# Moving the K projections three slots ahead in a three-pass attention stage, and one norm step on GpSimd ahead of a row of scatters

## The reference, cut to what matters

```python
scores = einsum('bthd,bshd->bhts', q, k * scale) + mask     # 16 heads of 8, mask: -10000 above the diagonal
context = einsum('bhts,bshd->bthd', softmax(scores), v)
for _ in range(3 - 1):
    context = _self_attention(context, k, v, mask)
out = context.reshape(B, S, 128) @ out_w.T + out_b
```

```python
w, idx = top_k(xf @ Wg, 2); w = softmax(w)
xhat = (xf - mean) * rsqrt(var + 1e-6)
h = relu((xhat * gamma[e] + beta[e]) @ W1[e] + b1[e]);  out = h @ W2[e] + b2[e] + xf
y = sum over the two chosen experts of w * out
```

## Time and profile before

| | |
|---|---|
| median of 3 runs | 4461.56 us (4457.56 to 4463.29) |
| the profiled execution: its own time | 4461.56 us |
| its span, first to last instruction | 4459.8 us |
| busy in the span: PE, DVE, ACT, POOL | 77%, 63%, 47%, 26% |
| mean granted TensorE clock | 0.867 of full |

### The profile page before, as it was taken

The page is one execution under the profiler, slowest core; times in us unless marked ns, Lnnn a source line. Parts: engine busy times, 40 slices in busy tenths (PEclk is TensorE's granted clock), DMA queues, the critical chain, the costliest instruction groups (busy, mean ns, idle before and its releaser), DMA issues. The chain is left out here.

```text
span 4459.8 us, 86703 instructions
## 1 busy us (share of the span) xinstructions
PE 3442.5 (77%) x30682; PEld 2229.3 (50%) x30682; DVE 2809.0 (63%) x7618; ACT 2089.4 (47%) x4656; POOL 1178.7 (26%) x2276
## 2 busy tenths in 40 slices
PE   5886888887888658739998989677982478869882
PEld 2443454463555338724454545344541456659872
DVE  4884675264887575537676777476756458955453
ACT  2664665223444435425666666453650134335551
POOL 2322221011111234530101010133320431234555
PEclk9987999797998679968999999788995599979996
DMA  5323331033220322221202021223312140122332
GB/s 95 56 32 55 54 56 24 15 94 44 36 37 14 57 70 67 74 49 25 45 20 41 24 38 28 38 51 55 58 29 62 50 122 19 51 69 86 90 82 63
DMA packets 317480, 231.40 MB, mean 52 GB/s; under 512 B 45379, under 2 KB 300960, under 8 KB 317004
## 3 DMA queue, kind: packets, MB, share of 16 engines
q1 hardware_dynamic: 304124, 199.36, 22.6%
q0 software_dynamic: 12928, 26.50, 2.0%
HBM read 68.43 MB, written 55.53 MB: 28 GB/s over the span
## 5 line engine op out<-in xcount | busy, mean ns | idle before, releaser
L1351 ACT ACTIVATE PT<-ps 128x512 f32<-128x512 f32 (+1 forms) x1600 | 812.0, 560 | 478.8 <-PE ps L1411 221.7
L1301 DVE TENSOR_REDUCE M<-ps 128x2 f32<-128x512 f32 x1024 | 655.3, 684 | 253.0 <-PE ps L1285 223.8
L1264 PE MATMUL ps<-SKB 49*128 49x256 bf16 (+2 forms) x3584 | 425.0, 276 | 150.2 <-DMA SKB<-HH 59.1
L1298 DVE TENSOR_REDUCE M<-ps 128x3 f32<-128x384 f32 x768 | 390.6, 550 | 190.4 <-PE ps L1282 125.4
L1446 PE MATMUL ps<-PT,VA 128*9 128x256 f32 (+1 forms) x7168 | 449.5, 370 | 1.4 <-ACT PT L1351 1.0
L3716 ACT ACTIVATE SKB<-ps,SKB 128x128 f32<-128x128 f32 x1032 | 294.6, 371 | 281.6 <-PE ps L3636 198.3
L1391 PE MATMUL ps<-SKB 51*128 51x256 bf16 (+2 forms) x3584 | 364.4, 268 | 63.1 <-DMA SKB<-MT 41.5
L3778 DVE COPY SKB<-SKB 128x1028 f32 (+1 forms) x258 | 186.0, 721 | 288.6 <-PE ps L3645 165.6
L1264 PEld LDWEIGHTS ps<-SKB 48*128 48x128 bf16 (+1 forms) x3584 | 138.0, 95 | 449.3 <-issue 161.9
L3645 PE MATMUL ps<-SKB 128*128 128x128 f32 x2064 | 288.8, 285 | 32.8 <-ACT SKB L3716 25.7
L3636 PE MATMUL ps<-SKB 128*128 128x128 f32 x2064 | 289.9, 286 | 0.0
(11 more groups left out here) (487 smaller groups left out, 6725.4 us busy)
## 6 DMA issues: line engine op xcount, KB each, us to landing
SKB<-HH SPq DMA_DIRECT2D x1224, 64.0 KB
SKB<-HH SPq DMA_DIRECT2D x576, 32.0 KB
PT<-L_sorted_rows SPq DMA_DIRECT2D x258, 64.0 KB
L_sorted_results<-SKB SPq DMA_DIRECT2D x258, 64.0 KB
SKB<-in_L3f_w SPq DMA_DIRECT2D x32, 256.0 KB
L_sorted_rows<-TV SPq DMA_DIRECT2D x2, 4032.0 KB, 29.2
SKB<-scratch SPq DMA_DIRECT2D x2, 2048.0 KB, 11.0
SKB<-in_L1f_w SPq DMA_DIRECT2D x16, 256.0 KB
```

The source lines that it names most:

```text
L1264: k = e.matmul(self.mx_bank(m + i)[:, o:o + n], K.QS[self.set(c)][64 * i:64 * i + rows, s, 256 * bb + 128 * qt:256 * bb + 128 * qt + 128], ...
L1298: k = e.tensor_reduce(K.M3[n % 2][:, hh, 0:3], mx[:, 0:384].rearrange("p (a k) -> p a k", a=3), axis=AX.X, op=ALU.max)
L1301: k = e.tensor_reduce(K.M3[n % 2][:, hh, 0:2], mx.rearrange("p (a k) -> p a k", a=2), axis=AX.X, op=ALU.max)
L1351: e.activation(K.PT[:, x % 4, n * i:n * i + n], self.st_bank(x, i)[:, 0:n], ACT.Exp, bias=0.0, scale=self.scale).then_inc(*self.exp.inc())
```

## The change

In the attention stage with three passes the K projection goes from 15 to 18 slots ahead of the chunk's first unit, and the copies of K from 12 to 15 slots ahead. All that hangs on these two numbers moves along: the projection and its read, the four instructions of the split, the 12 copies. Q and V stay. No other stage takes these branches (the other self attentions have rope, a gate or a cross part). In the experts stage `pool_root(e, 2)` is emitted ahead of the 24 scatters of part 1 and no longer behind the first 8. In the experts of layer L3 `normed` is false, and nothing changes.

```diff
-        self.Q, self.KP, self.V = ... else (-29, -27, -19) if gate else (-25, -15, -19)
-        self.QSTK, self.KSTK = (-26, -17) if cross else (-20, -12) if reps > 1 else (-14, -20) if gate else (-20, -14)
+        self.Q, self.KP, self.V = ... else (-29, -27, -19) if gate else (-25, -18, -19)
+        self.QSTK, self.KSTK = (-26, -17) if cross else (-20, -15) if reps > 1 else (-14, -20) if gate else (-20, -14)
...
         for _ in self.steps["pool"]:
             pass
+        if D.normed:
+            D.pool_root(e, 2)
         for h in (1, 2):
             begin, n = D.begins[h - 1], D.parts[h].tiles * top
             for i in range(n):
-                if D.normed and h == 1 and i == 8:
-                    D.pool_root(e, 2)
                 e.wait_ge(*self.xc.at(begin + i * min(n, D.parts[h - 1].NB - 1) // n))
                 self.pool_scatter(e, h, i)
```

More of the change, by code:

```diff
@@ L953, in __init__ @@
         self.OUT, self.TURN = self.OOS + 1, 6 if cross or gate else 5
-        self.Q, self.KP, self.V = (-30, -20, -13) if cross else (-29, -20, -19) if rope else (-29, -27, -19) if gate else (-25, -15, -19)
-        self.QSTK, self.KSTK = (-26, -17) if cross else (-20, -12) if reps > 1 else (-14, -20) if gate else (-20, -14)
+        self.Q, self.KP, self.V = (-30, -20, -13) if cross else (-29, -20, -19) if rope else (-29, -27, -19) if gate else (-25, -18, -19)
+        self.QSTK, self.KSTK = (-26, -17) if cross else (-20, -15) if reps > 1 else (-14, -20) if gate else (-20, -14)
         self.stack_slots = 3 if reps > 1 else 6
```

## The result

The changed kernel takes 4503.88 us, the median of 4 runs (4503.51 to 4506.82), against 4460.50 (4457.56 to 4463.29) of the kernel before in the same comparison: +43.4 us, a ratio of 1.0101, interval 1.0086 to 1.0115. The prediction had the sign, and in the attention stage the mechanism, but half the size: 4483, range to 4499. The profiled execution took 4495.31 us; in code that the change doesn't touch it was already 9.3 us ahead of the execution of before when the experts' blocks began, so stages are compared from their own starts. By the two traces the attention stage is 36.6 us longer from slot 32 to its last slot, and the stretch from the first block of the experts to slot 32 is 7.7 us longer.

What follows compares the result with a forecast made beforehand. It took the slot-by-slot round through PE, DVE and ACT, plus single stalls, to set the attention stage's pace. 17.9 + 2.1 + 0.9 - 1.2 + 1.7 = +21.4 on 4461.6 gave 4483 us; range 4477 to 4491, with rivals 4471 to 4499.

Steps and rivals of the forecast that it cites:

- the odd chunks: Attention stage: K's projection, three slots ahead, waits for DVE where it waited for ACT; 0.3 us each, +0.9 us.
- the start: Start of the attention stage: copies of chunk 1's K follow the first 36 without a gap and land sooner; -1.2 us.
- the moved root: Experts stage: all 24 scatters follow the root back to back, so the last, which releases block 23, is late; +1.7 us.
- DVE's seed: Experts stage: the root on POOL waits for this seed until 1699.96, so moving it ahead gives no gain.
- the landing: Attention: context 7's copies land 18.5 us after Q's, holding PE at slot 120 and in two other groups; +17.9 us.
- the clock: Attention stage: two stalls a group lower the granted clock; 0.7 us for each group, +2.1 us.
- three groups, even chunks, with the clock: Attention stage: PE held until context 7 lands in three groups, 17.9 us, plus 2.1 us for the lower clock.
- The first stall: Attention, slot 112: the context's `hi` waits some 8 us for Q's copies; alone it makes PE some 3.5 us late.
- the upper bound of 1.41: Experts stage: scatter pitch in us if DVE's SBUF copies hold back GpSimd's descriptors; the root term would be +3.3 us.
- Rival C: Attention: Q's copies land before slot 112, so neither split waits and three stalls go; -12.4 us, 4449 us; chance 4%.

Runs made afterwards that it cites:

- 8.0 alone: Against the kernel before, K's projection and copies three slots ahead for chunks 3, 5 and 7 only: +8.0 us (ratio 1.0024).
- 9.6 and 14.2 alone: Against the kernel before, only the root moved ahead of all 24 scatters, run on two chips: +9.6 us (1.0027) and +14.2 us (1.0031).
- even chunks' kernel: Against the kernel before, K's projection and copies three slots ahead for chunks 2, 4 and 6 only: +27.7 us (ratio 1.0073).
- The run with Q ahead: Changed kernel's K move, root as before, Q of chunks 2, 4, 6 projected, split and copied 8 slots earlier: +27.0 us (1.0052) against the kernel before.

## Why the prediction was wrong

The steps on the mechanism held: the wait passed from K to the context, two slots earlier; the context landed behind 24 copies; PE was held at slots 120, 216 and 312; the odd chunks, the start and the moved root had the signs given, and DVE's seed left no gain. What failed was four terms of the sum. The term for the experts stage held only the last scatter's delay and put at nothing what the row does to the blocks beside it; the term for the odd chunks was a difference of two waits and left out the projection itself; the landing was priced with a small packet at a quarter of a large one; and the clock was taken at 0.7 us a group. In us:

| term | predicted | measured |
|---|---|---|
| three groups, even chunks, with the clock | 17.9 + 2.1 | 27.7 alone (trace: 10.0, 8.2, 8.8, of which 8.2, 7.1, 7.1 up to slot 120) |
| K of the odd chunks | 0.9 | 8.0 alone (trace: 6.6) |
| start of the stage | -1.2 | -2.2 |
| experts stage | 1.7 | 9.6 and 14.2 alone (changed kernel's trace: 7.7) |

- **Landing.** The first stall alone made PE 3.3 us late in the first group of the even chunks' kernel (3.5 predicted), and the wait behind slot 119 added 4.9 (3.2 predicted). Up to slots 120, 216 and 312 the three groups lost 22.4 us, for 17.9. The issue times were right; the price of a small copy was not. I took 28 ns for its packets from a stretch in which the engines had gaps, and 120 from one in which they had a backlog. Small packets with a backlog, after:

```profile
DMA packets 182, 0.08 MB, mean 63 GB/s; under 512 B 23, under 2 KB 182, under 8 KB 182
...
q1 hardware_dynamic: 182, 0.08, 61.7%
```

  That is 2183.0 to 2184.3, where all data packets were of small copies: 0.617 x 16 x 1.3 us / 182 = 71 ns. A large packet in such a queue, before, 2165 to 2174, takes 127:

```profile
q1 hardware_dynamic: 646, 0.59, 57.1%
```

  The ratio is 0.56, not a quarter. Over the whole second row (2176 to 2193) the packets of 512 bytes took 57 ns and those of 1024 bytes 113, by the trace's packet records, and where the engines had gaps they took 31 (2154 to 2162) and 61 (2180 to 2182, before): about one half in either state. This is what the Trainium skill (DMA: Bandwidth & Descriptors, "Specifications") says of transfers of 512 bytes and up, and what I set aside on the word of two rows from unlike states. With that price the landing comes 20.4 us after Q's, measured 20.2, and the sum is 4489.
- **Clock.** From slot 120 to slot 136 another 1.7 us are lost in the first group (1.1 and 1.7 in the others), behind the dip to 0.52 above; 0.7 was taken for both stalls together. How much of it is the clock alone was not taken apart.
- **Odd chunks.** I priced the new place as a difference of two waits, 1.14 and 0.88. The projection had been nearly free at slot 129, where PE would else have waited for DVE; at slot 126 nothing covers it. The cost is the whole projection with its wait, 2.3 us, less 0.15 that slots 129 and 130 give back.
- **Experts stage.** The pitch of the row was forecast well: (1714.79 - 1695.34) / 15 = 1.30 us, for 1.33. Three scatters beside DVE's copies (L3778) took 1.02, 1.09 and 1.03 us, the others behind the first 0.97, so the upper bound of 1.41 was not reached. The row was 16 long and not 24, as the 17th waited for a block that was itself late. And PE's wait at block 23 was 4.20 us, for 5.8 predicted and 4.06 before: the path that the 1.7 stood for cost next to nothing. That such a row delays TensorE's signals, and with them blocks 12 to 15, was missing. The waits of the kernel before could have told it, in the stretch with the gathers (in total, times, longest):

```profile
ACT SKB L3716 <- remote: 18.7, 6, 5.5
DVE SKB L3778 <- remote: 17.7, 6, 4.7
```

- **Rival C** had another fault: with Q's copies early it need not have been 12 us faster, since a second wait, for the pair of maxima rows, ended at the same time. The run with Q ahead took both waits away at slot 116, and made two new ones at 108 and 124.

## What to carry to other kernels

Where a stall is named after one waiter, ask of every engine what it waited for at that moment, the weight loads too: of two waits that end together, taking away one gains nothing by itself. Price a transfer by rows from the state it will meet, a queue with a backlog or an idle one. And work moved out of a slot gives back only what nothing else in that slot would have taken.

## What the runs showed of the hardware

Beside unbroken rows of indirect DMAs on GpSimd, TensorE's semaphore signals came up to 14.4 us late and in bunches, on every chip of these runs but one, and in none of the four kernels profiled on that one. Where it happens the first experts stage has 33 to 41 signals over 0.1 us late, as long as its gathers go out in rows of 4 and 8; the trace lacks some of the updates, so these are least numbers. By the order of the blocks, with 7 scatters in the row the latest was 3.7 us behind its matmul's end, with 12 it was 8.3, and with 16 it was 14.0, 14.4 and 14.3; beside the gathers it was up to 7.5 in the kernel before. With one scatter in flight none was late. In the three-pass attention stage, which has no indirect DMA, none was late in any run. What holds them isn't shown by any row, and stays open.
